# Elimination, graph convolution and LSTM side by side: an earlier start and three and four products in turn

## The reference

```
h = relu(adj @ (h @ Wg0 + bg0)); h = relu(adj @ (h @ Wg1 + bg1))      # layer 0, graph convolution
for p in 1..4: the nodes in windows of p; an LSTM (own weights) runs over each
               window and its last hidden state replaces the window's last node
x += h
x += graph attention(relu(layernorm(x)))                              # layer 1
x += masked attention(relu(layernorm(x)))                             # layer 2
L = normalised Laplacian of adj; U = eigenvectors of L                 # layer 3
x += U @ (relu(U.T @ h @ W1 + b1) @ W2 + b2)
```

## Time and profile before

| | |
|---|---|
| median of 3 executions | 891.15 us (890.71, 891.15, 896.12) |
| the profiled execution | 895.78 us, its span 894.1 us |
| TensorE matmuls | 777.2 us busy, 87% |
| VectorE | 708.4 us busy, 79% |
| ScalarE | 501.8 us busy, 56% |
| GpSimd | 173.6 us busy, 19% |

### The profile page before, as it was taken

How to read it: one execution, slowest core, us unless ns; L and a number is a source line. 1 busy time by engine, 2 the same in 40 slices (tenths; PEclk the granted TensorE clock), 3 DMA queues, 4 the chain that set the end, 5 groups by cost and what they waited for, 6 DMA issues and landing times. The chain is left out here.

```text
span 894.1 us, 13697 instructions
## 1 busy us (share of the span) xinstructions
PE 777.2 (87%) x3730; PEld 519.0 (58%) x3738; DVE 708.4 (79%) x3420; ACT 501.8 (56%) x1106; POOL 173.6 (19%) x398
## 2 busy tenths in 40 slices
PE   3569998999999999999999996588875787788998
PEld 2358885445554566666555555466754565566665
DVE  6876777998888888898888778959779899859433
ACT  0017995665444344444444432288774796688675
POOL 3111111222221212221212110013112422270000
PEclk9999999999999999999999998699997998999999
DMA  9100000000000000000000000000000000000122
GB/s 274 44 1 1 1 2 0 1 1 0 1 0 1 1 0 1 1 1 2 0 1 1 0 1 1 0 1 1 1 1 0 1 1 1 1 1 1 48 71 71
DMA packets 13970, 12.16 MB, mean 14 GB/s; under 512 B 1091, under 2 KB 10822, under 8 KB 13894
## 3 DMA queue, kind: packets, MB, share of 16 engines
q1 hardware_dynamic: 10704, 8.46, 3.2%
q10 hardware_dynamic: 3190, 2.84, 1.1%
HBM read 7.10 MB, written 4.19 MB: 13 GB/s over the span
## 5 line engine op out<-in xcount | busy, mean ns | idle before, releaser
L566 ACT ACTIVATE G<-bank,bias 128x512 f32<-128x512 f32 (+1 forms) x252 | 159.2, 634 | 182.3 <-PE bank L663 159.1
L663 PE MATMUL bank<-HT,wih 128*128 128x512 f32 (+1 forms) x504 | 248.2, 579 | 0.4 <-ACT HT L552 0.4
L433 POOL TENSOR_TENSOR col_root<-sa,neg_half 128x1 f32<-128x1 f32 x126 | 69.3, 550 | 422.8 <-DVE sa L910 422.8
L663 PE MATMUL bank<-H,whh 128*128 128x512 f32 (+1 forms) x288 | 134.9, 550 | 1.2 <-DVE H L908 0.6
L522 ACT ACTIVATE T<-X,nbias,rstd 128x128 f32<-128x128 f32 x256 | 104.5, 484 | 4.9 <-DVE nbias L909 4.9
L526 ACT COPY T<-bank 128x512 f32<-128x512 f32 x128 | 75.1, 586 | 52.7 <-PE bank L663 38.5
L663 PEld LDWEIGHTS bank<-VI 128*128 128x128 f32 x254 | 47.4, 202 | 73.0 <-DVE VI L908 46.3
L663 PEld LDWEIGHTS bank<-HT,wih 128*128 128x128 f32 x504 | 80.2, 194 | 10.0 <-issue 3.9
L663 PEld LDWEIGHTS bank<-XI,A 128*128 128x128 f32 x252 | 45.2, 201 | 59.3 <-DVE A L909 50.4
L673 PE MATMUL bank<-ident,T 128*128 128x128 f32 x256 | 40.6, 288 | 41.4 <-ACT T L609 35.1
L909 DVE SCALAR_TENSOR_TENSOR XI<-xy,bank 128x2 f32<-128x2 f32 x125 | 28.2, 226 | 57.9 <-PE bank L663 51.8
(11 more groups left out here) (349 smaller groups left out, 1662.7 us busy)
## 6 DMA issues: line engine op xcount, KB each, us to landing
out_x<-T SPq DMA_DIRECT2D x16, 256.0 KB, 2.3
wih<-in_WihT ACTq DMA_DIRECT2D x1, 1024.0 KB
whh<-in_WhhT ACTq DMA_DIRECT2D x1, 1024.0 KB
qkvT<-in_WqkvT ACTq DMA_DIRECT2D x1, 192.0 KB
wg<-in_Wg ACTq DMA_DIRECT2D x2, 64.0 KB
l3w<-in_L3W ACTq DMA_DIRECT2D x2, 64.0 KB
adjT<-in_adjT ACTq DMA_DIRECT2D x1, 64.0 KB
adj<-in_adj SPq DMA_DIRECT2D x1, 64.0 KB, 2.0
```

The source lines that it names most:

```text
L433: e.tensor_tensor(out=col["root"][:, :], in0=sa[:, 0:1], in1=neg_half[:, :], op=ALU.pow).then_inc(root_ready, 1)
L566: e.activation(G[x.h][:, gate, 0:n], gate_bank(k)[:, 0:n], ACT.Tanh if gate == 2 else ACT.Sigmoid, bias=bias[:, 4 * (x.p - 1) + gate:4 * ( ...
L663: mm = lambda out, l, r, start=True, stop=True: e.matmul(out, l, r, start=start, stop=stop)
```

## The change

The graph convolution starts in step 5 instead of 10 and the LSTM products in 23 instead of 28. For 512 columns, window 3i takes two products only in odd steps (with one in each of the two other windows: three and four products in turn). Statistics are closed in two parts, 24 graphs in step 3 (stats_2 in 4) and 40 in step 8 (stats_2 in 9), ahead of the first group and of group 6. The one-off products move to steps 2 and 3, one place each, and ScalarE copies them out instead of VectorE. The masks are made at place 3 of steps 8 to 13, one instruction to a step. The two bias loads of the LSTM move to SP's queue behind x, with a semaphore of their own, as have wih and whh. All later parts of the statistics are numbered one higher (not shown).

```diff
 STATS_AT = 0
-PRE_AT = 6
-FINISH_AT = 8
-GRAPH_AT = 10
+PRE_AT = 2
+FIRST_ROWS = 24
+FINISH_AT = (3, 8)
+GRAPH_AT = 5
+MASKS_AT = 8
 LSTM_AT = GRAPH_AT + NG + 2

 def room(window, n):
-    return (3 if n < 400 else 2) if window % 3 == 0 else 1
+    if window % 3:
+        return 1
+    if n < 400:
+        return 3
+    return 2 if window // 3 % 2 else 1
...
-COLUMNS = {1: slice(0, B), 2: slice(0, B), ...
+COLUMNS = {1: slice(0, FIRST_ROWS), 2: slice(FIRST_ROWS, B), 3: slice(0, B), ...
...
 @blk.sync
+            e.dma_start(bl[:, 0, :], A_["bihT"]).then_inc(bl_in, 16)
+            e.dma_start(bl[:, 1, :], A_["bhhT"]).then_inc(bl_in, 16)
...
 @blk.scalar     # wih and whh on lstm_in instead of w_in, bl no longer here
+            def one_off():
+                e.wait_ge(pre_pe, 5)
+                e.copy(out=brow[0:1, 2, :], in_=bank[2][0:1, 0:P]).then_inc(pre_sb, 1)
+                e.copy(out=wa[:, :], in_=bank[3][:, 0:2]).then_inc(pre_sb, 1)
+                e.activation(mqk[:, :], bank[4][:, 0:P], ACT.Copy, scale=float(D) ** -0.5).then_inc(pre_sb, 1)
+                e.copy(out=wvo[:, :], in_=bank[5][:, 0:P]).then_inc(pre_sb, 1)
+                e.copy(out=b2rep[:, :], in_=bank[6][:, 0:P]).then_inc(pre_sb, 1)
+            def one_off_biases():
+                e.wait_ge(pre_pe, 7)
+                e.copy(out=bias0[:, :], in_=bank[3][:, ds(P, P)]).then_inc(pre_sb, 1)
+                e.copy(out=bias1[:, :], in_=bank[4][:, ds(P, P)]).then_inc(pre_sb, 1)
             for i in range(FIRST_MIXER_STEPS):
-                if i == FINISH_AT:
+                if i == PRE_AT:
+                    one_off()
+                    one_off_biases()
+                if i == FINISH_AT[0]:
                     root(1)
                     e.wait_ge(ln_rdy, 1)
                     ln(0, a_h)
...
                 if 0 <= g < NG - 1:
+                    if GB * (g + 1) == FIRST_ROWS:
+                        e.wait_ge(ln_rdy, 2)
                     ln(g + 1, a_h)
...
+                if i == FINISH_AT[1]:
+                    root(2)
...
 @blk.tensor
+            def one_off(part):
+                if part == 0:
+                    e.wait_ge(w_in, 16 * 14)
+                    mm(bank[2][0:1, 0:P], ones[:, 0:1], adjT[:, :]).then_inc(pre_pe, 1)
+                    mm(bank[3][:, 0:2], w1T[:, :], avec[:, :]).then_inc(pre_pe, 1)
+                if part == 1:
+                    mm(bank[4][:, 0:P], qkvT[:, 0, :], qkvT[:, 1, :]).then_inc(pre_pe, 1)
+                if part == 2:
+                    mm(bank[5][:, 0:P], qkvT[:, 2, :], wo[:, :]).then_inc(pre_pe, 1)
+                if part == 3:
+                    mm(bank[6][:, 0:P], ones[0:1, :], b2r[0:1, :]).then_inc(pre_pe, 1)
+                if part == 4:
+                    e.wait_ge(pre_sb, 5)
+                    mm(bank[3][:, ds(P, P)], brow[0:1, 2, :], brow[0:1, 0, :]).then_inc(pre_pe, 1)
+                    mm(bank[4][:, ds(P, P)], brow[0:1, 1, :], brow[0:1, 2, :]).then_inc(pre_pe, 1)
             def window(w):
                 i, place = divmod(w, 3)
                 g = i - GRAPH_AT
-                if i == PRE_AT and place == 0:
-                    one_off()
-                if i == PRE_AT + 2 and place == 0:
-                    one_off_biases()
+                one_off(w - 3 * PRE_AT)
...
 @blk.vector     # one_off and one_off_biases are gone, in their place:
+            def masks(part):
+                if part == 0:
+                    net(TS(gmask[:, :], adj[:, :], 0.0, NEG, ALU.is_equal, ALU.mult))
...              # parts 1 to 4: the four instructions of cmask, part 5: the LSTM biases' sum
             def first_mixer(i, place):
...
-                if place == 0 and i == PRE_AT + 1:
-                    one_off()
-                if place == 0 and i == PRE_AT + 3:
-                    one_off_biases()
-                if place == 0 and i == FINISH_AT:
-                    stats_1(1)
-                if place == 2 and i == FINISH_AT:
-                    stats_2(1)
+                if place == 3:
+                    masks(i - MASKS_AT)
+                for n, at in enumerate(FINISH_AT):
+                    if place == 0 and i == at:
+                        stats_1(n + 1)
+                    if place == 2 * n and i == at + 1:
+                        stats_2(n + 1)
```

More of the change, by code:

```diff
@@ L161, in half_list @@
         if k == NG // 2 + 2:
-            halves.append(("stats_2", 3))
+            halves.append(("stats_2", 4))
         if k == NG + 2:
-            halves.append(("stats_2", 4))
+            halves.append(("stats_2", 5))
         if k:
@@ L167, in half_list @@
         if k == NG // 2:
-            halves.append(("stats_1", 3))
+            halves.append(("stats_1", 4))
         if k == NG:
-            halves.append(("stats_1", 4))
+            halves.append(("stats_1", 5))
         if k == NG + NG // 2 + 2:
-            halves.append(("stats_2", 5))
+            halves.append(("stats_2", 6))
         if k == NG + NG // 2:
-            halves.append(("stats_1", 5))
-    return halves + [("stats_1", 6)]
+            halves.append(("stats_1", 6))
+    return halves + [("stats_1", 7)]
 class Group:
@@ L185, in __bool__ @@
         return 0 <= self.k < GROUPS
-COLUMNS = {1: slice(0, B), 2: slice(0, B), 3: slice(0, B // 2), 4: slice(B // 2, B), 5: slice(0, B // 2), 6: slice(B // 2, B)}
+COLUMNS = {1: slice(0, FIRST_ROWS), 2: slice(FIRST_ROWS, B), 3: slice(0, B), 4: slice(0, B // 2), 5: slice(B // 2, B), 6: slice(0, B // 2), 7: slice(B // 2, B)}
 HALF = half_list()
@@ L202, in needs @@
     if S >= NG - 2:
-        h = max(h, HALF.index(("stats_2", 3)) + 1)
+        h = max(h, HALF.index(("stats_2", 4)) + 1)
     if S >= NG + NG // 2 - 2:
-        h = max(h, HALF.index(("stats_2", 4)) + 1)
+        h = max(h, HALF.index(("stats_2", 5)) + 1)
     return h
-for _n in (3, 4, 5):
+for _n in (4, 5, 6):
     ROOTS_AFTER[max(S for S in SLOTS if needs(S) <= HALF.index(("stats_1", _n)) + 1)] = _n
@@ L351, in build @@
         prod = HTf[:, ds(4608, 2048)]
-        c_adj, w_in = sems("c_adj w_in")
+        c_adj, w_in, bl_in, lstm_in = sems("c_adj w_in bl_in lstm_in")
         x_in = [sem(f"x_in{k}") for k in range(4)]
@@ L513, in _ @@
             e.dma_start(avec[:, :], A_["aT"]).then_inc(w_in, 16)
[L514 to L517, removed]
+            e.dma_start(wih[:, :, :, :], A_["WihT"].rearrange("s h (g o) -> h s g o", g=4)).then_inc(lstm_in, 16)
+            e.dma_start(whh[:, :, :, :], A_["WhhT"].rearrange("s h (g o) -> h s g o", g=4)).then_inc(lstm_in, 16)
             def ln(g, done):
@@ L596, in signs @@
                     e.activation(sg[n % 2][:, 0:w], (prodL if b == NB - 1 else prod)[:, 0:w], ACT.Sign).then_inc(sgn_ready, 1)
-            root(2)
-            e.wait_ge(ln_rdy, 2)
+            root(3)
+            e.wait_ge(ln_rdy, 3)
             for S in SLOTS:
@@ L632, in _ @@
                     if not after.gat and after.g % (NG // 2) == 0:
-                        e.wait_ge(ln_rdy, 3 + after.g // (NG // 2))
+                        e.wait_ge(ln_rdy, 4 + after.g // (NG // 2))
                     ln(after.g, g_h if after.gat else q_h)
                 if S == GROUPS - 2:
-                    e.wait_ge(ln_rdy, 5)
+                    e.wait_ge(ln_rdy, 6)
                 if GROUPS - 2 <= S < GROUPS:
@@ L646, in _ @@
                 if 2 * it == NG // 2:
-                    e.wait_ge(ln_rdy, 6)
+                    e.wait_ge(ln_rdy, 7)
                 for g in pair:
@@ L654, in _ @@
                 if not it:
-                    root(6)
+                    root(7)
                 for g in pair:
@@ L734, in window @@
                             e.wait_ge(a_out, NG)
+                            e.wait_ge(lstm_in, 32)
                         if q == 0 and x.needs is not None:
@@ L940, in stats_2 @@
                 STT(nbias[:, o], mean[:, o], -0.5, rstd[:, o], ALU.mult, ALU.mult).then_inc(ln_rdy, 1)
[L942 to L961, removed]
+            def masks(part):
+                if part == 0:
+                    net(TS(gmask[:, :], adj[:, :], 0.0, NEG, ALU.is_equal, ALU.mult))
+                if part == 1:
+                    net(TS(cmask[:, :], upper[:, :], NEG, None, ALU.mult))
+                if part == 2:
+                    net(TT(sq[:, :], ones[:, :], upper[:, :], ALU.subtract))
+                if part == 3:
+                    net(TT(sq[:, :], sq[:, :], adj[:, :], ALU.mult))
+                if part == 4:
+                    net(TT(cmask[:, :], cmask[:, :], sq[:, :], ALU.add))
+                if part == 5:
+                    e.wait_ge(bl_in, 32)
+                    net(TT(bias[:, :], bl[:, 0, :], bl[:, 1, :], ALU.add))
             def first_mixer(i, place):
@@ L1209, in _ @@
                 residual(g)
-            stats_1(2)
+            stats_1(3)
             e.wait_ge(wy_ps, 23)
             TT(QT[:, :], ident[:, :], bank[1][:, 0:P], ALU.subtract).then_inc(wy_dv, 1)
-            stats_2(2)
+            stats_2(3)
```

(2 more changed lines are left out.)

## The result

| | before | changed |
|---|---|---|
| median | 892.49 us (4 executions, 890.71 to 896.12) | 882.18 us (4, 876.14 to 883.54) |
| ratio | | 0.9873, 95% interval 0.9837 to 0.9909 |
| profiled execution, span | 895.78, 894.1 | 882.39, 880.4 |

A second measurement of the changed kernel, on another chip, gave 0.9861 (0.9832 to 0.9889; medians 881.70 against 893.56). The change makes the kernel 1.3% faster; 881 us was forecast, within 872 to 893, and faster by over 1% held a chance of 0.47.

What follows compares the result with a forecast made beforehand. The first ten steps were taken to hang on VectorE and the elimination's round trip, LSTM steps on TensorE. Start -21.8, LSTM steps +11.2, tail +0.6 gave -10.0: 885.8 us profiled, 881 median, range 872 to 893.

Steps and rivals of the forecast that it cites:

- The start: Steps 0 to 22, up to the first LSTM step: 112.0 us in place of 133.76, that is -21.8.
- Held steps: LSTM steps where VectorE runs f*c and c+ig ahead of u: nine with three products, at 4.20 us each.
- Free three-product steps: LSTM steps of three products, not delayed by f*c and c+ig: 25 at 3.60 us and 8 at 3.48.
- The clock after step 60: Behind nearly empty LSTM step 60: 1.0 us added for a slow TensorE clock.
- signs of being wrong: Step 3 over 7.5 us, steps 7 to 9 over 6, or clock under 1 after step 52, 60 or a held one.
- The rival that every held or empty step is followed by such a drop: LSTM steps: 11 held or empty ones each followed by a 1.9 us clock drop, +21, so 902 us; chance 0.08.
- Steps 66 to 97: Steps 69 to 100 of before (336 columns) come back with the same pattern, 119.0 us.
- The tail: Behind step 125: one product more, +0.9 us for TensorE, 0.3 hidden by VectorE's tridiagonal work: +0.6.
- The masks: Five mask instructions and the bias sum, one to a step from 8 to 13: they cost nothing.
- the cover: TensorE's eight adjT products and wg1's, lasting until about 2.5 us, hide the masks; without it they cost some 1.8.
- the start gives less: Rival: first steps slower through a later clock rise (+4.5 us) or ScalarE's chain in step 3; about 886 us; chance 0.25.
- the held steps are not held: Rival: the 9 held and 2 empty LSTM steps cost 3.6 us, -6.5 more, 874.5 us; chance 0.13.

Runs made afterwards that it cites:

- the list: Changed kernel with four products in a written list of steps instead of odd steps; ratio to before 0.9803, repeated 0.9788 (median 875.49 us).
- f*c moved: Changed kernel with f*c at place 2 (ahead of sa) instead of place 3 (ahead of u); ratio to before 0.9931, with the list as well 0.9887.

## Why the prediction was right, by its own steps

| step | forecast us | measured us |
|---|---|---|
| 0 to 2 | 13.6 | 13.58 |
| 3 / 4 | 6.3 / 5.7 | 5.91 / 5.69 |
| 5 / 6 / 7 | 6.2 / 6.3 / 5.4 | 6.28 / 5.52 / 5.60 |
| 8 / 9 | 5.05 / 5.75 | 4.87 / 5.44 |
| 10 to 20 | 49.9 | 49.4 |
| 21, 22 | 7.8 | 7.81 |
| sum 0 to 22 | 112.0 | 110.1 |
| 23 | 6.15 | 6.07 |
| 24 to 65 and 98 to 124 | 271.7 | 269.8 |
| 66 to 97 | 119.0 | 120.2 |
| tail | +0.6 | 0.0 |
| change of the profiled time | -10.0 | -13.4 |

- **The start** was 1.9 us better than forecast. In step 3 stats_1 moved u by 1.14 us (1.25 was priced), and of the bias products 0.2 showed, not 0.5: from u to the next power it took 3.59 us, in the steps before 3.41. Step 6 was 0.8 better because the products became fast late in it (eight that start at 44.56 took 1.50 us, in the second execution of the same kernel 2.08) and not in step 7; that is a matter of the execution, four others had 6.3 there. Step 10 took 4.09 instead of 4.54, which I had not seen: VectorE held step 9 so long that TensorE entered step 10 with its products done and waited 0.39 us for A.
- **Held steps** came out as priced (4.20): steps 56, 58, 104, 106, 108, 110, 122 and 124 took 4.11 to 4.26, and 113 took 4.38. The two nearly empty ones, 52 and 60, took 4.26 and 4.12. (The expectations for f*c count 52 among the nine held ones and leave out 113.) This term was the least certain and kept the gain of the turn small. Free three-product steps in the last batch were better than the 3.48 taken from one row: 3.34 to 3.46 but for one at 3.7, as step 112 shows beside the four-product step 117.

```profile
464.88:468.23 3.35, 0.54 (x1) 1.00 0.00 0
483.85:488.06 4.21, 0.55 (x1) 1.00 0.00 0
```

- **The clock after step 60** was foreseen (1.0 us) and cost 1.7. (A drop had been priced at 1.9 from step 28; step 23 with it and without it, in the changed kernel's two executions, gives 1.5.) It was also one of the prediction's own signs of being wrong (a clock under 1 in the step after 52, 60 or a held one), and that sign came: 0.72 in step 61. The prediction contradicts itself here; its sum was right to have the term. The rival that every held or empty step is followed by such a drop did not come: there was one, where TensorE had a single product of the LSTM in a step. The held steps with three products were followed by none.
- **Steps 66 to 97** took 1.2 us more than the 119.0 forecast. Three of them (70, 80, 96) were 0.2 to 0.35 longer than their like before; in step 96 VectorE stood 0.38 us between two of its own instructions. Why stays open.
- **The tail** did not grow; the extra product hid behind VectorE's tridiagonal work altogether.
- **The masks** cost nothing, as said, but the cover named was too wide in step 9.
- The rival "the start gives less" did not come in the profiled execution, but its mechanism is real: with the products fast only from step 7 on the start is 1.0 to 2.5 us longer, as in four other executions. The rival "the held steps are not held" is refuted by the lengths of these steps, by the list and by f*c moved.

The medians' gain of 10.3 is as forecast, and that it agrees to 0.3 us is luck: the sum was made against the profiled pair, which differs by 13.4, 3.4 more than it. Of these 1.9 are the start, 0.6 the tail, 0.8 the LSTM steps with step 23, and the rest what follows. Nor is a difference of that size above the spread of executions: the changed kernel's times alone spread by 7.4 us. What was right is the make-up of the sum, and above all the held steps.

## What to carry to other kernels

A planner that spreads one engine's work evenly over steps should ask which steps another engine makes long anyway: work put there is free. Here the even turn brought the loop's end 3 us forward, and the list, which put the work there and left no step thin, another 7 (of which 4.5 to 6.2 reached the whole time). Work moved out of a place must be priced where it lands: f*c cost 0.7 us ahead of u and 0.4 to 0.6 ahead of sa. And a step that is left with a single product is paid for in the next one, where TensorE runs at half rate (1.7 us here, in all five executions).

## What the runs showed of the hardware

- The moment at which TensorE's products become fast after a quiet start is not fixed: for the same first 35 us it lay at 41 us in one execution and at 53 in another, which moves the power of step 10 by up to 3.6 us. In three executions the granted clock rose early and fell once more (0.71 to 0.76 in step 6).
- The clock column reads 1.00 at the start though the products last twice as long (2.06 us for eight against 1.14). The traces have no clock record there: the first one begins at 72.5 us before and at 45.3 in the changed kernel, about where the products become fast, and a stretch without a record is printed as 1.00. So at the start the durations have to be read, not the column. At steps 23 and 61 it does read 0.72.
- Step 23, the first with LSTM products behind two light steps (4.11 and 3.70 us), took 6.04 to 6.29 us at a clock of 0.72 or 0.73 in eight executions with this start and 4.60 at 1.00 in three, among them the second one of the changed kernel. That does not go with an early or late start: the three had the power of step 10 at 61.39, 63.84 and 66.33 us. A comparison by the power of one step can mislead by 2 us; lengths of the steps that an edit touches are steadier (within 0.02 us between the two executions of the changed kernel, but for steps 6, 7 and 23).
